# Linear attention's key bias: from an add on VectorE to a bf16 product on TensorE

## The reference

```
k = (x @ Wk + bk).reshape(b, n, H, DH)
k_prime = jnp.exp(jnp.einsum('bnhd,df->bnhf', k, wk_feat))
k_sum = k_prime.sum(axis=1)
context = jnp.einsum('bnhf,bnhd->bhfd', k_prime, v)
```

## Time and profile before

| | |
|---|---|
| three plain runs | 2104.21, 2099.49, 2098.7 us; median 2099.49 us |
| profiled execution, its own time | 2113.85 us |
| span in its profile | 2112.0 us |
| mean granted TensorE clock | 0.862 |
| stage la_k | about 79.3 to 177.9 us |

### The profile page before, as it was taken

One profiled execution on the slowest core, in us unless ns is written; L12 is line 12 of the kernel. 1 busy time (PEld: TensorE's weight loads), 2 busy tenths in 40 slices (PEclk: granted clock), 3 DMA queues, 4 the chain that ended last, 5 costly groups with the idle time before them and its releaser, 6 DMA issues. The chain is left out here.

```text
span 2112.0 us, 33478 instructions
## 1 busy us (share of the span) xinstructions
PE 1636.7 (77%) x12275; PEld 785.5 (37%) x12287; DVE 1256.8 (60%) x2588; ACT 899.9 (43%) x1728; POOL 476.1 (23%) x404
## 2 busy tenths in 40 slices
PE   2658984599888888884757989849957988859997
PEld 1446542234333333332323444334423434243333
DVE  3212237777668666844167888154476888048888
ACT  1012333266566565562423666612224666622221
POOL 0320242766556655630030000000010000000000
PEclk7567996599989999897877999869967999769999
DMA  6012204775666566530042110000051010000000
GB/s 187 26 62 67 70 24 151 187 188 142 164 155 167 151 160 165 145 99 11 25 126 46 31 32 17 1 1 0 7 167 45 18 32 17 1 1 0 0 0 20
DMA packets 211250, 153.62 MB, mean 73 GB/s; under 512 B 57449, under 2 KB 192025, under 8 KB 210970
## 3 DMA queue, kind: packets, MB, share of 16 engines
q1 hardware_dynamic: 202426, 135.35, 24.6%
q10 hardware_dynamic: 6624, 12.06, 1.9%
q0 software_dynamic: 2048, 4.20, 0.7%
HBM read 83.47 MB, written 67.37 MB: 71 GB/s over the span
## 5 line engine op out<-in xcount | busy, mean ns | idle before, releaser
L1814 DVE TENSOR_REDUCE a1a_partial<-a1a_room 128x4 f32<-128x1024 f32 x192 | 225.9, 1220 | 31.1 <-PE a1a_room L1879 30.5
L1773 ACT ACTIVATE a1a_probsT<-a1a_st 128x512 f32<-128x512 f32 (+1 forms) x416 | 205.3, 577 | 20.3 <-PE a1a_st L1912 19.8
L2236 ACT ACTIVATE a3a_probsT<-a3a_st 128x512 f32<-128x512 f32 (+2 forms) x320 | 155.3, 562 | 118.7 <-PE a3a_st L2298 74.1
L2236 ACT ACTIVATE a2a_probsT<-a2a_st 128x512 f32<-128x512 f32 (+2 forms) x320 | 155.4, 561 | 109.3 <-PE a2a_st L2298 67.1
L2153 DVE TENSOR_REDUCE a3a_maxima<-a3a_room 128x2 f32<-128x1024 f32 (+3 forms) x160 | 170.2, 1113 | 35.2 <-PE a3a_room L2269 23.4
L2153 DVE TENSOR_REDUCE a2a_maxima<-a2a_room 128x2 f32<-128x1024 f32 (+3 forms) x160 | 170.2, 1113 | 28.5 <-PE a2a_room L2269 19.1
L1949 PE MATMUL a1a_ctx<-a1a_probsT,a1a_vpad 128*9 128x512 f32 (+3 forms) x1408 | 149.0, 523 | 1.5
L1678 POOL TENSOR_TENSOR a1a_shifted<-a1a_shifted,a1a_best 128x1024 f32<-128x1024 f32 x64 | 121.6, 1901 | 105.1 <-DVE a1a_best L1820 105.0
L1879 PE MATMUL a1a_room<-stack 48*128 48x128 bf16 (+1 forms) x1376 | 111.0, 270 | 43.6 <-DVE a1a_partial L1814 22.8
L1810 DVE CUSTOM_DVE_ANT_0 a1a_shifted<-a1a_room,a1a_bands 128x256 f32<-128x256 f32 x256 | 93.5, 421 | 84.6 <-PE a1a_room L1879 79.3
L1776 ACT ACTIVATE a1a_probsT<-a1a_st 128x512 f32<-128x512 f32 x128 | 73.7, 602 | 129.4 <-PE a1a_st L1921 129.3
(11 more groups left out here) (495 smaller groups left out, 3327.3 us busy)
## 6 DMA issues: line engine op xcount, KB each, us to landing
a1a_bands<-a_band SPq DMA_DIRECT2D x112, 192.0 KB, 4.0
a_near<-a1a_shifted SPq DMA_DIRECT2D x112, 192.0 KB, 3.0
a1a_near<-a_near SPq DMA_DIRECT2D x64, 256.0 KB, 4.1
a_band<-a1a_r_mix SPq DMA_DIRECT2D x64, 254.0 KB, 3.6
stack<-q SPq DMA_DIRECT2D x96, 96.0 KB
stack<-k SPq DMA_DIRECT2D x32, 96.0 KB
l_inputs<-l_zeros SPq DMA_DIRECT2D x1, 2624.0 KB, 9.4
f_x<-l_inputs SPq DMA_DIRECT2D x8, 320.0 KB, 5.5
```

The lines of the kernel that those rows point to most:

```text
L1773: nc.scalar.activation(dst, src, ACT.Exp).then_inc(exp_done, 1)
L1814: nc.vector.tensor_reduce(partial[:, g % 2, :, 1 + r].rearrange("p (a s) -> p a s", a=2), src, X_AXIS, ALU.max).then_inc(job_free, 1)
L2236: nc.scalar.activation(probsT[:, block_at % BLOCK_ROOMS, place:place + heads, lo:], src, ACT.Exp).then_inc(exp_done, 1)
```

## The change

TensorE adds the bias of the keys to the logits in PSUM, by a second product that accumulates onto the first. `bkf` is split into three bf16 parts whose sum is the f32 value: partitions 0 to 31 of `bias_parts` hold the first part, 32 to 63 the second, 64 to 95 the third. `share` is 96 x 128 of 1/32, so the product of `share` and `bias_parts` sums 32 equal rows of each part, each divided by 32: the bias, on every token. ScalarE then reads the logits in PSUM. VectorE makes the parts once, in eight instructions at the start of the block, for which TensorE waits before the first bias product; it has nothing more to do in the loop. The buffer `biased` goes. TensorE writes the logits of tile t+1 after the exponential of t-1 rather than after the add of t-1.

```
-            biased, kprime = pk.sb("biased", [P, 2, H * F]), pk.sb("kprime", [P, 2, H * F])
-            logits, biased_ready, k_ready, k_used = pk.sem("logits"), pk.sem("biased"), pk.sem("k"), pk.sem("k_used")
+            kprime = pk.sb("kprime", [P, 2, H * F])
+            bias_parts, bias_rest, share = pk.sb("bias_parts", [96, H * F], BF16), pk.sb("bias_rest", [96, H * F]), pk.sb("share", [96, P], BF16)
+            logits, bias_steps, k_ready, k_used = pk.sem("logits"), pk.sem("bias_steps"), pk.sem("k"), pk.sem("k_used")
...
                     def key_logits(t):
                         if t >= 2:
-                            pe.wait_ge(biased_ready, t - 1)
-                        nc.tensor.matmul(logit[t % 2][:], k.xnT[:, t * P:(t + 1) * P], wkf[:], start=True, stop=True).then_inc(logits, 1)
+                            pe.wait_ge(k_ready, t - 1)
+                        nc.tensor.matmul(logit[t % 2][:], k.xnT[:, t * P:(t + 1) * P], wkf[:], start=True, stop=False)
+                        if t == 0:
+                            pe.wait_ge(bias_steps, 8)
+                        nc.tensor.matmul(logit[t % 2][:], share[:], bias_parts[:], start=False, stop=True).then_inc(logits, 1)
...
                 @block.vector
                 def _(dve):
-                    for t in range(NT):
-                        dve.wait_ge(logits, t + 1)
-                        if t >= 2:
-                            dve.wait_ge(k_ready, t - 1)
-                        nc.vector.tensor_tensor(biased[:, t % 2, :], logit[t % 2][:], bkf[:], ALU.add).then_inc(biased_ready, 1)
+
+                    chain = Chain(dve, bias_steps)
+                    chain(nc.vector.memset(share[:], 1.0 / 32), nc.vector.tensor_copy(bias_parts[:], bkf[0:96, :]))
+                    chain(nc.vector.tensor_tensor(bias_rest[32:64, :], bkf[32:64, :], bias_parts[32:64, :], ALU.subtract),
+                          nc.vector.tensor_tensor(bias_rest[64:96, :], bkf[64:96, :], bias_parts[64:96, :], ALU.subtract))
+                    chain(nc.vector.tensor_copy(bias_parts[32:64, :], bias_rest[32:64, :]), nc.vector.tensor_copy(bias_parts[64:96, :], bias_rest[64:96, :]))
+                    chain(nc.vector.tensor_tensor(bias_rest[64:96, :], bias_rest[64:96, :], bias_parts[64:96, :], ALU.subtract))
+                    chain(nc.vector.tensor_copy(bias_parts[64:96, :], bias_rest[64:96, :]))
...
                 def _(act):
                     for t in range(NT):
-                        act.wait_ge(biased_ready, t + 1)
+                        act.wait_ge(logits, t + 1)
                         if t >= 2:
                             act.wait_ge(k_used, t - 1)
-                        nc.scalar.activation(kprime[:, t % 2, :], biased[:, t % 2, :], ACT.Exp).then_inc(k_ready, 1)
+                        nc.scalar.activation(kprime[:, t % 2, :], logit[t % 2][:], ACT.Exp).then_inc(k_ready, 1)
```

## The result

Twenty runs of each kernel, taken together: the kernel after takes 2113.78 us (median; 2104.11 to 2126.38), the kernel before 2103.77 us (2096.36 to 2115.27). The ratio is 1.0047, 95% interval 1.0030 to 1.0065, so the change makes the kernel slower by 6 to 14 us. Forecast were +5 us and 2104.5 us on the base of the first three runs of before; on the base of the twenty the same +5 us would be 2108.8.

What follows compares the result with a forecast made beforehand. The path through la_k's loop and finish was the bound, TensorE in steady tiles. Stall 3.7, bias products 0.43 and 1.3, loop end -0.55 gave +4.9: forecast +5 us, 2104.5 us; 8-in-10 range 2095 to 2113.

Steps and rivals of the forecast that it cites:

- Start: Head of la_k: TensorE waits for the split of the bias, first gram products at 86.1 instead of 82.88, +3.2 us.
- The upper bound: Start of la_k: three subtractions stretched beside GpSimd's scatters add 3.3 us more, so +6.5 us at most.
- Bias product: TensorE in la_k's loop, one per tile: 0.43 us at the lower clock, 0.21 at full clock.
- End of the loop and resumption: la_k's loop without VectorE's add: about 0.7 us saved at the resumption, 0.55 at the last tile, together -1.25 us.
- Through the stall: la_k's loop while GpSimd works: the kernel after falls between one and two tiles behind, +3.7 us.
- case (i): Stall in la_k: same tile when GpSimd ends, start and bias products of tiles 0 to 7 hidden; -0.7, sum +0.5 us.
- 127.4: Sign in the profile after: TensorE resuming after the stall before 127.4 us would mean case (i).
- If nothing stalled: Whole la_k loop at the steady pace: start +3.2, bias products 3.4, less 0.55 at the end: +6.1 us.
- The change touches only the stage la_k: Premise: only la_k, from 79.3 us to the barrier after 177.9 us, is affected.
- R2: Rival: slower beyond 0.3%, 2106 to 2112 us, by a start beyond +3.4 without stall or two tiles of arrears; chance 0.35.
- R3: Rival: la_k's stall goes with VectorE, 2070 us or part of it; chance 0.10, plus 0.03 for small clock gains.

Runs made afterwards that it cites:

- seven_after: The kernel after with stage la_k run seven times, scatters in turns 0, 2, 4 and 6: 2615.77 us, against 2602.10 for the kernel before run likewise.
- late_after: The kernel after with GpSimd's 32 scatters issued only after the last gram copy: ratio 0.9980 to the kernel before.
- filler: The kernel before with 16 small unread products at the head of TensorE's list in the experts' block, in a 5.8 us wait: ratio 1.0041.
- early16: The kernel before with 16 small products (32 instructions) in the router's block, where TensorE waits 13 us for a load: ratio 1.0031, repeated 1.0023.
- after112: The kernel after with 112 small products in the router's wait, TensorE's list 256 instructions longer than before: ratio 1.0008 to the kernel before, repeated 1.0015.
- late_before: The kernel before with GpSimd computing its tables first and issuing the 32 scatters only after the last gram copy: ratio 0.9946.
- early64: The kernel before with 64 small products (128 instructions) in the router's block, where TensorE waits for a load: ratio 1.0012.
- early128: The kernel before with 128 small products (256 instructions) in the router's block, where TensorE waits for a load: ratio 0.9985.
- one_split: The kernel before with only the bias split and TensorE's wait for it added, parts unused, VectorE still adding: ratio 1.0014.
- one_nobias: The kernel after without split and bias product, so the logits lack the bias: ratio 1.0020 to the kernel before.

## Why the prediction was wrong

- **Start, +3.2 us.** Right: 86.12 against 82.88. The split took 79.45 to 83.53, worked out for 79.25 to 83.55. The cast is a fast one (0.36 us for 96x512) and the subtractions weren't stretched beside the scatters (0.68 us); the two casts of 32x512 take 0.99 together, the last one alone 0.42. The prediction read from the Trainium skill (SBUF — State Buffer, Who interferes with whom) that beside the two-input subtractions nothing in the stage should hold anyone up; it passed over the casts, which the section also counts among the instructions that can contend with GpSimd. The upper bound held a slip: stretched by 3.14/1.22, subtractions of 1.29 + 0.69 us are 3.1 longer, not 3.3.
- **Bias product, 0.21 us in a steady tile.** Right (0.22), and 0.43 at the lower clock (85.69 to 86.12).
- **End of the loop and resumption, -1.25.** Right: -0.70 and no gap at the last tile.
- **Through the stall, +3.7.** Wrong: case (i), which I had as the lower bound (-0.7), is what happened, and TensorE resumed at 126.72, before the 127.4 that was named as a sign of it. Tile 6 waited for GpSimd's end in both kernels, so start and early bias products were hidden. With it the stage's sum is +0.5; the profile has +0.6, and over six turns with scatters each, read from the profiles, the means are 98.8 us before and 98.7 after.
- **If nothing stalled, +6.1.** Near: +4.6 in seven_after, +5.0 in late_after.
- **The change touches only the stage la_k.** This is the step that failed. The sum of the stage is 0.5 us, and the measured loss is 6 to 14. I took every part behind the barrier for a shifted copy of itself. In its place the runs show a cost outside the stage: 16 idle products, which add as many instructions to TensorE's list as the bias products do, cost 6.9 us (1.3) with a stage as long as before (filler, early16, early16_b), and after112 takes 7.6 us (2.1) back from the change. With it goes a lower granted clock (0.865 against 0.872 on average over the runs); in which stage most of it falls the profiles don't tell.
- **The size.** Of the 9.3 us between 2104.5 and 2113.78, 4.3 are the base (2099.49 from three runs, 2103.77 from twenty) and 5.0 the effect. That the forecast came as near as half is luck: three quarters of its +5 are the +3.7 for a stall that added nothing. That the time came near my R2 in size is a coincidence too: R2's mechanism (a start beyond +3.4 us, two tiles of arrears) did not occur.
- **R3, the stall goes with VectorE.** Fell: 34.9 us of waits without source remain, ScalarE's now. It goes with the scatters, as the turns without them and late_before show.

What stays open: how 32 instructions lead to a lower clock. The page of the kernel after has a queue for instructions (queue, kind: packets, MB, share) whose size fits TensorE's list:

```profile
q8 instruction: 94, 1.54, 0.3%
```

1.54 MB in 94 packets is 16384 bytes each, for some 25,000 TensorE instructions; in the profiles of early64 and early128 there are 95 packets. The Trainium skill (Runtime: NRT & Kernel Launch, Instruction fetch mechanics) gives 256 instructions to such a block and calls the crossing of a block mostly hidden. That 256 more cost nothing and 32 more do fits the size of a block; whether the 6.9 us speak against "mostly hidden" is open, as the trace names no wait as one for instructions: that the fetch is the path was not shown. A rival stands untested: that any edit of any engine's list can move the time by some microseconds, as one_split and one_nobias (+4.2, error 1.8) suggest, and that early128 and after112 happened to come out low. Open too are the 2.6 us (error 1.7) left to after112. Whether TensorE's products end late beside the scatters or only the news of it was not tried.

## What to carry to other kernels

Before pricing work that is put on an engine in a loop, ask what the loop really waits for: here 36 us of stall beside GpSimd's indirect DMAs hid 5 us of added work, and moving the scatters (0.9946) is worth more than the edits of the arithmetic tried here (leaving the bias out gave 1.0020). An effect below half a per cent must be looked for in several profiles of the same stage (the stage repeated in one program is the cheapest way) and held against a control that only lengthens the instruction list; without the control, the 10 us would have been put down to the bias product. And a control of this size needs many runs: twelve of them leave an error of 2 us. Work removed from an engine off the path is worth what its leaving uncovers at the ends of the loop, here 1.5 to 2.4 us a turn for split, add and bias together.

## What the runs showed of the hardware

- Beside GpSimd's 32 indirect DMAs a loop of TensorE, VectorE and ScalarE takes 68.5 us instead of 32.5, and finish 49.9 instead of 30.5, though neither waits for the other's data. The Trainium skill (SBUF — State Buffer, Who interferes with whom) has TensorE and ScalarE never waiting for anyone at SBUF's ports; here, while GpSimd works, VectorE is free from 115.36 for logits whose records end at 103.05 and adds at 126.02. Through which path is not known.
- Sixteen products in idle time, 32 instructions more in TensorE's list, cost 6.9 us of 2104 (error 1.3, 36 runs); 128 products, 256 instructions, cost none (-2.7, error 2.1, 12 runs). The cause isn't shown.
- The same kernel gives either of two lengths of one stage, by the granted clock: 284.0 and 274.4 us for the third layer's attention in two profiles of the kernel after.
- An f32 to bf16 cast within SBUF of 96x512 takes 0.36 us, about half of the add of 512 columns (0.69); two casts of 32x512 beside the scatters took 0.99.
